# One core, a gated two-layer block: 128-row score matmuls, scores one half step ahead, expert weights turned earlier, first loads reordered

## What is computed

```python
x = x + tanh(g_xattn[0]) * L0_xattn(layernorm(x), ctx, mask, Wq, Wk, Wv, bq, bk, bv)
x = x + tanh(g_ffn[0])   * L0_ffn(layernorm(x), router_w, gate_w, up_w, down_w)
x = x + tanh(g_xattn[1]) * L1_xattn(layernorm(x), ctx, mask_bk)
x = x + tanh(g_ffn[1])   * L1_ffn(layernorm(x), gate_up_proj, down_proj)

# L0_xattn: q, k, v = W @ x + b;  softmax(q k^T / sqrt(8) + mask) v     (8 heads of 8, 256 x 256)
# L0_ffn, over all tokens, 8 experts of width 512, top-p routing weights w:
for e in range(8):
    out += (silu(x @ gate_w[e].T) * (x @ up_w[e].T)) @ down_w[e].T * w[:, e:e + 1]
```

## Time and profile before

| | |
|---|---|
| median of 3 runs | 1066.92 us (1066.81 to 1067.99) |
| profiled execution: its time | 1070.54 us |
| profiled execution: its span | 1068.80 us |
| PE busy | 869.6 us, 81% of the span |
| DVE busy | 742.1 us, 69% |
| ACT busy | 576.8 us, 54% |
| POOL busy | 565.3 us, 53% |
| mean granted TensorE clock | 0.906 of 2.4 GHz |
| DMA moved | 122.67 MB, mean 115 GB/s |

### The profile page before, as it was taken

How to read it: one execution, slowest core, us unless ns; L and a number is a source line. 1 busy time by engine, 2 the same in 40 slices (tenths; PEclk the granted TensorE clock), 3 DMA queues, 4 the chain that set the end, 5 groups by cost and what they waited for, 6 DMA issues and landing times.

```text
span 1068.8 us, 25000 instructions
## 1 busy us (share of the span) xinstructions
PE 869.6 (81%) x9015; PEld 686.4 (64%) x9015; DVE 742.1 (69%) x2490; ACT 576.8 (54%) x1258; POOL 565.3 (53%) x568
## 2 busy tenths in 40 slices
PE   2447677778999999999999999999999867866564
PEld 1224445556777777777777777777777756755464
DVE  1566777466877787787877778787777586565552
ACT  1357675445666676666666667666674213222222
POOL 4256454344777768676676867667664222221110
PEclk9855559799999999999999999999999989988877
DMA  4679996463767686677866777775764120000100
GB/s 137 168 148 237 212 218 158 110 122 67 143 126 146 120 141 132 132 147 133 138 122 132 138 125 146 133 138 118 130 106 71 59 91 11 20 23 21 32 20 21
DMA packets 319520, 122.67 MB, mean 115 GB/s; under 512 B 274716, under 2 KB 312612, under 8 KB 319396
## 3 DMA queue, kind: packets, MB, share of 16 engines
q1 hardware_dynamic: 319396, 121.07, 56.2%
HBM read 45.53 MB, written 8.39 MB: 50 GB/s over the span
## 4 chain that ended last, share of the span: by engine, by line
PE 49%; DVE 19%; ACT 9%; issue 8%; POOL 6%; DMA 5%; SPq 2%; POOLq 0%; DVEq 0%; ACTq 0%
PE psU L735 14%; PE psY L735 11%; PE psG L735 7%; PE ps L735 4%; PE psV L735 4%; DMA p_turn<-p_parts 4%; PE psT L735 3%; DVE ps L1081 3%; POOL hp_lo L520 2%; ACT p L618 2%; ACT p_parts L626 2%; PE psM L735 2%; POOL p_parts L528 2%; DVE th_ga_h L1176 2%; PE psV L895 2%
## 5 line engine op out<-in xcount | busy, mean ns | idle before, releaser
L528 POOL TENSOR_TENSOR p_parts<-p,p_parts 128x512 f16<-128x512 f32 x256 | 296.0, 1157 | 180.9 <-ACT p_parts L626 163.7
L520 POOL TENSOR_TENSOR hp_lo<-th_ga_h,hp_hi 128x512 f16<-128x512 f32 x128 | 149.0, 1164 | 171.0 <-ACT hp_hi L650 171.0
L735 PE MATMUL psU<-xT,w_gu 128*128 128x256 f16 x1536 | 195.6, 279 | 44.3 <-DVE th_ga_h L1176 32.3
L735 PE MATMUL psG<-xT,w_gu 128*128 128x256 f16 x1536 | 194.7, 278 | 14.6 <-issue 4.6
L735 PEld LDWEIGHTS psU<-xT,w_gu 128*128 128x128 f16 x1536 | 143.0, 99 | 87.9 <-DVE th_ga_h L1176 41.2
L735 PE MATMUL psY<-w_dn,hp_hi 128*128 128x256 f16 x1024 | 185.3, 276 | 11.1 <-POOL hp_lo L520 11.1
L735 PEld LDWEIGHTS psG<-xT,w_gu 128*128 128x128 f16 x1536 | 143.7, 99 | 54.7 <-issue 30.1
L618 ACT ACTIVATE p<-psT,exp_bias 128x256 f32<-128x256 f32 x256 | 107.2, 470 | 112.1 <-DVE exp_bias L1085 111.9
L626 ACT ACTIVATE p_parts<-p 128x512 f16<-128x512 f32 x256 | 161.6, 631 | 7.4 <-DMA p_turn<-p_parts 6.3
L1081 DVE CUSTOM_DVE_ANT_0 ps<-ps,mask_in 128x256 f32<-128x256 f32 x256 | 104.2, 448 | 84.4 <-PE ps L735 83.5
L618 ACT ACTIVATE p<-ps,exp_bias 128x256 f32<-128x256 f32 x256 | 107.2, 470 | 96.8 <-DVE exp_bias L1085 96.0
(11 more groups left out here) (154 smaller groups left out, 1109.1 us busy)
## 6 DMA issues: line engine op xcount, KB each, us to landing
mask_in<-in_mask_Bx2048x_ff SPq DMA_DIRECT2D x32, 256.0 KB, 3.1
part_scratch<-parts SPq DMA_DIRECT2D x16, 384.0 KB, 3.1
q_stack<-part_scratch SPq DMA_DIRECT2D x64, 96.0 KB
k_stack<-part_scratch SPq DMA_DIRECT2D x64, 96.0 KB
stage<-in_L_ffn_gate_w SPq DMA_DIRECT2D x8, 512.0 KB, 4.4
stage<-in_L_ffn_up_w SPq DMA_DIRECT2D x8, 512.0 KB, 4.4
stage<-in_L_ffn_down_w SPq DMA_DIRECT2D x8, 512.0 KB, 4.7
p_turn<-p_parts SPq DMA_TRANSPOSE x256, 3.4
```

What stands on the lines that cost most here:

```text
L520: pool.tensor_tensor(hp_lo[:, u % 2, :], hb32[:, u % 2, :], hp_hi[:, u % 2, :], ALU.subtract).then_inc(s["h_split"], 1)
L528: pool.tensor_tensor(p_parts[:, g % 4, 1, :, :], p32[:, g % 3, :, :], p_parts[:, g % 4, 0, :, :], ALU.subtract).then_inc(s["plo_done"], 1)
L735: return pe.matmul(out_, lhsT, rhs, start=start, stop=stop, skip_group_check=shares_bank)
```

## The change

- `q_stack` has a further dimension for the half of the heads. Each half's rows lie in their old partitions and all other partitions are zero, so `scores` multiplies all 128 rows. `k_stack` is set to 1.0 once. The two zeroing memsets of `q_stack` are on DVE.
- `scores(0)` stands ahead of the loop. In half step `g`, `scores(g + 1)` stands between gate or up and down.
- The 48 weight pieces are numbered. Eight (`W_AHEAD`) are turned before the loop, then one in each half step (`weight_at`), the last in `g = 39`. Stage loads: six ahead of the loop, then one every second half step. The first unit waits for all pieces; the other waits of units for pieces go, also those of the transposes for `gate_used` and `up_used`.
- `p32` has two buffers; `exps(g)` waits for `low_done(g - 2)`.
- First loads: the weights Wq and Wk lead on SP, then the first x rows, context 0, Wv, mask 0, three weight stages, context 1, mask 1; the rest of x follows two pieces of stack loads. The biases, the router and the gates go out from ACT, each group with its own semaphore. ACT also issues half of the first pair's stack loads, after four weight copies.
- The first q/k cut is on DVE instead of POOL; the gates' tanh and the router's turn come later; the statistics of x are all in step 0.

The diff, cut to its core:

```diff
+W_PIECES = 6 * NE
+W_AHEAD = 8
...
-        q_stack = eb("q_stack", [P, 2, 2, 4, D], BF16)
+        q_stack = eb("q_stack", [P, 2, 2, 2, 4, D], BF16)
-        p32 = eb("p32", [P, 3, 2, 256], F32)
+        p32 = eb("p32", [P, 2, 2, 256], F32)
...
+        def weight_at(g):
+            w = W_AHEAD + g
+            return (w // 6, w % 6 // 2, w % 2) if w < W_PIECES else None
...
+        def load_stacks(eng, par, q, piece):
+            eng.wait_ge(s["parts_stored"], 16 * (q + 1))
+            if q < 2:
+                eng.wait_ge(s["stacks_set"], 2)
+                eng.wait_ge(s["q_zeroed"], q + 1)
...
# SP
-                    if n < NE and i in (2, 4, 6):
-                        load_weight_stage(n + 1, i // 2 - 1)
+                    if i % 2 == 0 and 6 + g // 2 < 3 * NE:
+                        load_weight_stage(6 + g // 2)
...
+            load_small_weight(0, "wst_loaded")
+            load_small_weight(1, "wst_loaded")
+            sp.dma_start(x_res[:, 0:2, :], x_d[:, 0:2, :]).then_inc(s["x01_loaded"], 16)
+            sp.dma_start(ctx_in[:, 0, :], ctx_d[0]).then_inc(s["ctx0_loaded"], 16)
+            load_small_weight(2, "wv_loaded")
             load_mask(0, 0)
+            for c in range(3):
+                load_weight_stage(c)
+            sp.dma_start(ctx_in[:, 1, :], ctx_d[1]).then_inc(s["ctx1_loaded"], 16)
             load_mask(1, 1)
+            store_parts(0, 0)
+            for piece in range(2):
+                load_stacks(sp, 0, 0, piece)
             sp.dma_start(x_res[:, 2:16, :], x_d[:, 2:16, :]).then_inc(s["x_loaded"], 16)
-            store_parts(0, 0)
-            for piece in range(4):
-                load_stacks(0, 0, piece)
             store_parts(1, 1)
+            for c in range(3, 6):
+                load_weight_stage(c)
...
# POOL
+            pool.memset(k_stack[:, :, :, :, :], 1.0).then_inc(s["stacks_set"], 1)
             pool.memset(v_parts[:, :, :, :, :], 1.0).then_inc(s["stacks_set"], 1)
-            for piece in range(4):
-                cut_qk(0, piece)
...
# ACT
-            act.wait_ge(s["small_loaded"], 16 * N_SMALL)
-            act.activation(gates[:, :], gate_in[:, :], ACT.Tanh).then_inc(s["gates_ready"], 1)
+            (six DMAs: b_q, b_k, b_v, router, two gates)
+            act.wait_ge(s["brow_loaded"], 32)
...
-                if g >= 3:
-                    act.wait_ge(*low_done(g - 3))
+                if g >= 2:
+                    act.wait_ge(*low_done(g - 2))
...
             copy_qk(0)
             copy_qk(1)
+            act.wait_ge(s["gate_loaded"], 32)
+            act.activation(gates[:, :], gate_in[:, :], ACT.Tanh).then_inc(s["gates_ready"], 1)
+            for w in range(W_AHEAD // 2):
+                w_high(w // 6, w % 6 // 2, w % 2)
+            for piece in range(2, 4):
+                load_stacks(act, 0, 0, piece)
+            for w in range(W_AHEAD // 2, W_AHEAD):
+                w_high(w // 6, w % 6 // 2, w % 2)
...
# PE
-                u = unit_at(e, m, 0)
-                if u:
-                    pe.wait_ge(s[("gate_used", "up_used")[k]], u)
...
-                    last = mm(score_bank(g)[:, nt, :], q_stack[64 * hh:64 * hh + 56, par, b2, hp, nt * P:nt * P + P],
-                              k_stack[64 * hh:64 * hh + 56, par, b2, hp, :])
+                    last = mm(score_bank(g)[:, nt, :], q_stack[:, par, hh, b2, hp, nt * P:nt * P + P],
+                              k_stack[:, par, b2, hp, :])
...
-                if tile == 0:
-                    pe.wait_ge(s["w_split"], 2 + copies)
-                    if ip == 0:
-                        pe.wait_ge(s["w_split"], 2 + 6 * (e + 1))
+                if u == 0:
+                    pe.wait_ge(s["w_split"], 2 + W_PIECES)
...
+            for w in range(W_AHEAD):
+                weight_transposes(w // 6, w % 6 // 2, w % 2)
...
-                    if g < 8 * B:
-                        scores(g)
-                    if n < NE and hp < 3:
-                        weight_transposes(n, hp, half)
-                        copies += 1
+                    w = weight_at(g)
+                    if w is not None:
+                        weight_transposes(*w)
                     (gate or up)
+                    if g + 1 < 8 * B:
+                        scores(g + 1)
                     if u2 is not None:
                         unit_down(u2, half)
...
+            scores(0)
             for n in steps:
                 step(n)
...
# DVE
+            dve.memset(q_stack[:, 0, :, :, :, :], 0.0).then_inc(s["q_zeroed"], 1)
...
             norm1(0)
+            dve.wait_ge(s["qk_copied"], 2)
+            (the q/k cut of pair 0, four instructions)
+            dve.wait_ge(s["bias_v_loaded"], 16)
             bias_to_v(0)
             norm1(1)
+            dve.memset(q_stack[:, 1, :, :, :, :], 0.0).then_inc(s["q_zeroed"], 1)
+            for w in range(W_AHEAD):
+                w_low(w // 6, w % 6 // 2, w % 2)
```

More of the change, by code:

```diff
@@ L527, in p_low @@
                     pool.wait_ge(*turned(g - 4))
[L528 removed]
+                pool.tensor_tensor(p_parts[:, g % 4, 1, :, :], p32[:, g % 2, :, :], p_parts[:, g % 4, 0, :, :],
                                    ALU.subtract).then_inc(s["plo_done"], 1)
@@ L584, in _ @@
                                ACT.Copy).then_inc(s["bias_turned"], 1)
-            act.wait_ge(s["wst_T"], 3)
             act.wait_ge(s["consts_ready"], 3)
             for w in range(3):
+                act.wait_ge(s["wst_T"], max(2, w + 1))
                 for b2 in range(2):
                     rows = slice(S * b2, S * b2 + S)
-                    src = psM[rows, w * S:w * S + S]
+                    src = psM[rows, w * S:w * S + S] if w < 2 else psY[rows, 1, 0:S]
                     if w < 2:
@@ L625, in p_high @@
                     act.wait_ge(*turned(g - 4))
-                act.activation(p_parts[:, g % 4, 0, :, :], p32[:, g % 3, :, :], ACT.Copy).then_inc(s["phi_done"], 1)
+                act.activation(p_parts[:, g % 4, 0, :, :], p32[:, g % 2, :, :], ACT.Copy).then_inc(s["phi_done"], 1)
             def x_high(q):
@@ L749, in _ @@
                 pe.transpose(psV[:, w:w + 1], bias_turn[:, w, :], ident[0:1, 0:1]).then_inc(s["biasT_ready"], 1)
-            for k in range(KT):
-                last = pe.transpose(psY[:, 0, k * NE:k * NE + NE], rt_in[:, k * P:k * P + P], ident[0:NE, 0:NE])
-            last.then_inc(s["router_T"], 1)
             def weight_transposes(e, m, k):
@@ L889, in _ @@
             project_qk(1, 1)
+            for w in range(W_AHEAD):
+                weight_transposes(w // 6, w % 6 // 2, w % 2)
+            pe.wait_ge(s["rt_loaded"], 16)
+            for k in range(KT):
+                last = pe.transpose(psY[:, 0, k * NE:k * NE + NE], rt_in[:, k * P:k * P + P], ident[0:NE, 0:NE])
+            last.then_inc(s["router_T"], 1)
             def late_turn(src, done):
@@ L985, in step @@
                 ja, jb = late_at(n)
-                copies = 6 * min(n, NE)
                 for i in range(8):
                     g, hp, half = 8 * n + i, i // 2, i % 2
-                    if g < 8 * B:
-                        scores(g)
-                    if n < NE and hp < 3:
-                        weight_transposes(n, hp, half)
-                        copies += 1
+                    w = weight_at(g)
+                    if w is not None:
+                        weight_transposes(*w)
                     u0, u2 = unit_at(n, hp, 0), unit_at(n, hp, 2)
@@ L1296, in step @@
                         maxima(g)
-                    if n < NE and hp < 3:
-                        w_low(n, hp, half)
+                    w = weight_at(g)
+                    if w is not None:
+                        w_low(*w)
                     if half == 0:
```

121 lines of the change are left out of this document (57 added, 64 removed).

## The result

The changed kernel takes **1013.58 us** (median of 4 runs, 1011.03 to 1014.37) against 1066.87 of the kernel before beside it: ratio 0.9504, interval 0.9472 to 0.9536. The gain is 53 us, where 92 were forecast. 1013.58 lies outside the range, 1.6 above its end.

What follows compares the result with a forecast made beforehand. PE's instruction stream was taken as the steady limit, DVE next. Gains 36.5 (rows) + 13 (order) + 47.6 (steps 5 to 7) + 4 (start) - 8 (steps 0 to 4) = 93, rounded 92: 1066.9 to 975 us, range 950 to 1012.

Steps and rivals of the forecast that it cites:

- 24 x 8 x 0.19 = 36.5 us: Steps 8 to 31: 128-row scores remove 0.19 us of gaps per half step, gaining 36.5 us; other bound nothing.
- What is late next is POOL's hp_lo. A steady step becomes 23.2 - 1.5 - 0.55 = 21.1: Steps 8 to 31: 1.5 us a step from 128 rows, 0.55 from fewer PE waits; POOL's hp_lo limits next.
- The order of the scores: Steps 8 to 31: scores one half step ahead cut PE's waits, gaining 13 us; bounds 30 gained, 24 lost.
- Steps 5 to 7: Weights done before the first unit: three steps fall from 111.0 to 63.4 us, gain 47.6; bounds 16.4 and 50.
- Steps 0 to 4: Two more pieces and one more stage load a step lose 8 us; bounds nothing or 28.
- The sign that I named for a wrong prediction: Prediction is wrong if, among other signs, PE waits for a stage load in steps 0 to 4.
- The start: Until the first scores: first projection starts at 7.4, scores at 29.5, gain 4 us; bounds 4 lost, 7 won.
- the start hardly moves: Rival: small packets hold the DMA engines whoever issues them; start gains 2.4 instead of 7, so 980 us; chance 0.08.
- DVE did not become the bound: Rival for the steady steps: DVE's clumped work raises stalls from 0.7 to 1.7 us a step, 999 us; chance 0.13.
- the gap stays: Rival: gaps around score matmuls belong to a semaphore wait or the bank, not rows; 1011 us; chance 0.12.
- the head gives it back: Rival: steps 0 to 4 lose 28 us and steps 5 to 7 gain only 32; 1011 us; chance 0.12.
- The slower p32 case: Rival: with two p32 buffers exps wait for POOL's p_low, 26.4 us a step, 1118 us; chance 0.03.

Runs made afterwards that it cites:

- e1: The changed kernel with the score matmuls reading 56 rows again, q_stack still split and zeroed: 1018.79 us, ratio 0.9531 to the kernel before.
- the square of four kernels: The changed head with 128 or 56 score rows, each in new or old score order: 1013.58 and 1018.79 us (new), 1042.03 and 1049.66 us (old).
- e9: The changed kernel with each pair's twelve stack loads issued over seven half steps from 5 on, instead of three in each of four: 987.87 us, ratio 0.9256.
- e5: The changed kernel with 128 rows kept but the scores of g back ahead of the gate or up matmuls of g: 1042.03 us, ratio 0.9742.
- e10: The changed kernel with ACT issuing value bias, router and gates only once Wq and Wk are turned: 1010.35 us, ratio 0.9466.
- e3: The changed kernel with POOL's memsets of k_stack and v_parts moved ahead of the first power: 1008.04 us, ratio 0.9426.
- e4: The changed kernel with the load of x's other 14 blocks issued behind the fourth weight stage: 1006.00 us, ratio 0.9414.
- e11: The changed kernel with six weight pieces turned ahead of the loop instead of eight, loop stage loads one half step later: 1007.85 us, ratio 0.9443.
- e7: The changed kernel with 56 rows, three p32 buffers and the old q_stack: 1018.13 us, ratio 0.9515.

## Why the prediction was right or wrong

**128 rows: mechanism right, value wrong.** The gap belongs to the row count (e1 against the changed kernel: 0.1 on each side, nothing else changed). The Trainium skill's rule on tiling modes (TensorEngine Tiling (Array Packing), Key Properties), that a change of mode drains TensorE, agrees with this. The step that failed is "24 x 8 x 0.19 = 36.5 us" as a gain: PE's stream did get 37 us shorter, but time removed from the stream is not time gained. The other bound, nothing, was tied to the wrong question, whether the gap goes. It goes, and the square of four kernels still gives 5 to 8 us. DVE's product and POOL's hp_lo came too late once in each step already, and a stream that is 1.5 us a step shorter meets them, and SP's transposes, earlier. What the rows are worth once SP's queue is in order stays open: 56 rows with the plan of e9 were not run.

**"What is late next is POOL's hp_lo. A steady step becomes 23.2 - 1.5 - 0.55 = 21.1": this step cost the most, 19.6 us.** The 1.5 came true in the bare step (21.21 to 19.66). The 0.55 did not: the delays, which were to fall, rose from 1.99 to 2.32. Late next was SP's queue: 3.37 us in each of four half steps of a pair, against PE's 2.59 before and 2.39 after. The same loads stood there in the kernel before, and cost PE 2.4 us; I counted the DMA engines' share and DVE's time, but not the time of SP's issues. e9 shows it, since it changes nothing but the half steps of those loads: its delays are 1.58, 0.41 below those of before. With it the forecast's 21.1 comes out at 21.24.

**The order of the scores: under-sized.** 13 us forecast, 22 to 25 measured. I took all waits from 1.26 to 0.7 a step. The listed wait for psU went from 0.70 to only 0.60, but hp_lo's went altogether, against my expectation that it would be late next. With 128 rows in the old order (e5) psG's, 0.2 a step, and many short ones would have come on top, and the new order takes those away too.

**Steps 5 to 7: right in size.** 67.7 against 63.4, a little above the 60 to 66 that I gave, at a granted clock of 0.95. e9's 64.0 shows that 3.7 of the missing 4.3 are SP's queue again.

**Steps 0 to 4: right in sign, too large.** 3.8 lost instead of 8. The sign that I named for a wrong prediction did show: PE waits 20.9 us for stage loads there, in 10 waits. It was a poor sign, since the stretch, with the DMA engines busy 0.91 of the time, still took less than forecast.

**The start: wrong by 15.4 us, beyond its bounds (4 lost, 7 won).** Two steps of it failed. The projection started 15.74 - 7.4 = 8.3 us late, and from there to the first scores it took 29.3 us where the forecast had 22.1. "The projection starts at 7.4" overlooked that ACT's small packets hold SP's loads (the rival "the start hardly moves" had the mechanism; I gave it 0.08, on a DMA share of 0.11 that says nothing of the order in a queue), and the memset of k_stack, which I had not counted among those of the change: its 3.51 us on POOL, and v_parts' 1.43 behind it, stand beside DVE's xn. e10 and e3 show the two: 2.4 and 3.7 us at the scores. That the fourth stage lands behind x's 1.8 MB was the lower bound, with 4 us; it came true and PE waited 12.27. e4 takes 6.2 of them away. e11 shows the alternative: not to need that stage before the scores.

**The rivals.** The gap did not stay. DVE did not become the bound: psU's stall stayed at 0.6 a step. The time of 1013.58 lies by chance beside the two rivals at 1011; neither "the gap stays" nor "the head gives it back" is what happened, though the start is part of the head. The slower p32 case is refuted by the time itself; its sign, that ACT waits for POOL's p_parts, did show (11.6 us), and e7 finds no cost behind it, with 56 rows. Three buffers with 128 rows were not run.

**The range** reached to 1012 because each rival took one mechanism away. Two unseen losses, the queue (19.6) and the start (15.4), added up.

## What to carry to other kernels

Time that is taken out of the busiest engine's stream is a gain only as far as each of its suppliers has slack: before counting it, add up for every engine and every issuing queue, SP's too, what it does in the most crowded half step, not on average, and compare that with the new length of the half step. When work is started one half step earlier, its inputs are needed one half step earlier: move their loads too, and no further than their buffers allow. At the start, look at what the waiting engines' neighbours do in that time, since an earlier load can put two instructions side by side that never met.

## What the runs showed of the hardware

- POOL's memsets of k_stack and v_parts (3.51 and 1.43 us) held DVE's 128x256 tensor-scalar from 0.41 to 4.37 us (4.87 in e10).
- Two 56-row matmuls among 128-row ones cost 0.1 us ahead and 0.1 behind (e1: 1.41 for 1.31, 0.32 for 0.22).
- The issue of one transpose takes SP 1.27 us, that of a stack load 0.47 to 0.70. The stage load issued next behind x's 1.8 MB took 5.62 us to issue, in e4 5.18; in e4 the one ahead of x took 0.54.
- Four small loads on ACT's queue (1 to 64 KB) delayed SP's loads of 32 and 256 KB by 3 us (Wk at 7.39 against 4.05, x at 8.26 against 5.26).
- A recorded wait of 0.48 us for psU lengthened the distance of two matmuls' starts by 0.65.
- In steps 0 to 4 a granted clock of 0.79 (e1) instead of 0.61 changed nothing: 118.1 and 117.8 us.
